# Layer 0's recurrence: the scan's input product on GpSimd beside a 1024-element sum, and the key softmax finished first

## The chip, the cores and the metric

The kernel runs on one core of one Trainium2 chip. The metric is the device time of one execution in microseconds (us); before the change the median of three runs is 1492.85 us (1488.32 to 1498.87). The five engines of a core run their own instruction streams and meet at semaphores: PE (TensorE, with PEld its weight loads), DVE (VectorE), ACT (ScalarE), POOL (GpSimd) and SP (which issues DMAs).

## The reference, cut to what matters

Two layers, each a mixer and a mixture of experts (MoE), on `[8, 512, 128]` float32. The change lies in the mixer of layer 0, a recurrence over 32 chunks of 16 tokens. Each of the 8 x 16 = 128 pairs of batch and head has two small weight matrices, `W_in` and `W_out`, of 4 x 8 elements, which are carried from chunk to chunk:

```
k_h = softmax_D(k_t . W_in) * lr_t[..., 1:]
q_h = softmax_D(q_t . W_in)
o_t = q_h . W_out + (mask(q_h k_h^T)) v_t
W_out = W_out + sum_n k_h[n] v[n]
for _ in range(2):
    g_out = -attn(W_in, k_t, v_t)
    g_in  = -attn(W_out, v_t, k_t)
    W_in  = W_in  - lr_in  * g_in
    W_out = W_out - lr_out * g_out
```

The masked product and `q_h . W_out` together are `q_h` times the running sum of `W_out + k_h v` over the tokens of the chunk, so the kernel makes a scan over the products `k_h v` and never forms the 16 x 16 matrix. After the recurrence come a layer norm per head, a gate, an output projection, the gathered result of the MoE, and layer 1.

## The kernel before, in words

The 128 pairs of batch and head lie on the 128 partitions. All of a chunk's work is on the free axis: 4 states (D) x 8 elements (e) x 16 tokens (l) = 512 elements, and 1024 where two weight matrices are taken as a pair.

One chunk is one call of `step(c, ...)` in the DVE block. It runs c = 0 alone, then three loops (c = 1, 2; c = 3 to 26; c = 27 to 30), then c = 31 alone. The 24 steps of the middle loop are called routed: during them PE and ACT also compute layer 0's MoE, three 128-token tiles a step, and DVE makes one 128x512 product for each tile (L1534, `gated`). In the routed steps GpSimd makes two of the recurrence's products, `q_product` (PQ, L446) and `o_product` (OP, L451), each 128x512. In the other eight steps DVE makes both itself, because GpSimd is issuing the indirect DMAs that scatter the MoE's input (L640, during c = 0 to 2) or gather its output (L675, from c = 27).

Order within DVE is kept by a counter, the class `Order`: `o.mark(...)` lets an instruction raise the counter when done and returns its number, `o.wait(n)` waits for that number. So an instruction whose operand has just been made waits for the instruction before it, and one that is independent of it is issued at once. Values that other engines make or need have semaphores of their own.

The part of a step that the change touches is its opening, up to the scan. The names are those of the code:

- `z_3` (L1542): sums of the pair's exponentials E3, 128 to 8 elements. `g_3` (L1547): the pair's product G3 = VV * E3, 1024 elements. `z_k` (L1549): sums of the key exponentials EK, 64 to 16 elements. `r_3`, `r_k` (L1551, L1553): reciprocals.
- `s_3` (L1555): the sum over the 1024 elements of G3 into 64 of GR. `l_k` (L1557): 16 elements of ZK times the learning rate. `n_3` (L1559): the 64 sums times the reciprocals Z3. `h_k` (L1561): EK times ZK, which finishes the key softmax.
- `w_c` (L1566): the new `W_out` into the first column of SC. `x_k` (L1568): the scan's input product V * EK, 512 elements, into the other 16 columns of each row of SC. `run` (L1571): the scan over SC, 544 elements, into CS.

After the scan the step computes the pair of scores with the new `W_out` (L1605 to L1611), the query softmax, the pair for `W_in` (L1615 to L1632), the scores for the next chunk (L1636 to L1644). Three gated products lie between. The exponentials are made on ACT (L1140), E3 before EK. The function `red` is DVE's tensor_reduce, `tt` its tensor_tensor, and `bc` makes a broadcast view.

GpSimd's stream in the routed steps is a loop: `o_product(c)`, then `q_product(c + 1)`. It waits for the query softmax of chunk c and then for the product at L1636, which DVE makes with the scores of chunk c + 1.

Of the kernel before, what the change touches and what calls it, by code (L numbers as in the profile page):

```python
# [9 lines left out]
ALU = mybir.AluOpType  # L10
ACT = mybir.ActivationFunctionType
AX_X = mybir.AxisListType.X

P = 128
B, L, D = 8, 512, 128
# [3 lines left out]
H, HD, DI, CH = 16, 8, 4, 16  # L19
# [13 lines left out]
FIRST = 3  # L33
# [5 lines left out]
def bc(ap, axis, n):  # L39

    a = ap.unsqueeze(axis)
    shape = list(a.shape)
    shape[axis] = n
    return a.broadcast_to(shape)

def flat(a):

    return a if len(a.shape) == 2 else a.rearrange("p a b -> p (a b)") if len(a.shape) == 3 else a.rearrange("p a b c -> p (a b c)")
# [55 lines left out]
def build(nc, d):  # L105
# [5 lines left out]
    with ExitStack() as ctx:  # L111
        def sb(name, shape, dt=F32):
            return ctx.enter_context(nc.sbuf_tensor(name, shape, dt))

        def sem(name):
            return ctx.enter_context(nc.semaphore(name))
# [41 lines left out]
        V = sb("V", [P, HD, L])  # L158
# [37 lines left out]
        G2, G3 = (r.take(2 * DI, HD, CH) for _ in range(2))  # L196
# [5 lines left out]
        SC, CS = r.take(DI * HD, CH + 1), r.take(DI * HD, CH + 1)  # L202
        EK, EQ = r.take(DI, CH), r.take(DI, CH)
        VV = r.take(2, HD * CH)
# [3 lines left out]
        S2, S3, E2, E3 = (r.take(2 * DI, CH) for _ in range(4))  # L208
# [5 lines left out]
        MK, MQ, ZK, ZQ = (sb(n, [P, CH]) for n in ("MK", "MQ", "ZK", "ZQ"))  # L214
        M2, M3, Z2, Z3 = (sb(n, [P, 2 * DI]) for n in ("M2", "M3", "Z2", "Z3"))
        GR = sb("GR", [P, 4, DI * HD])
# [90 lines left out]
        v_pair = sem("v_pair")  # L307
# [3 lines left out]
        op_ready = sem("op_ready")  # L311
        p3_ready = sem("p3_ready")
        qh_ready = sem("qh_ready")
        o_ps = sem("o_ps")
        o_copied = sem("o_copied")
        xg_loaded = [sem(f"xg_loaded{k}") for k in range(TPS)]
# [127 lines left out]
        def pq_of(eng, c):  # L444

            return eng.tensor_tensor(PQ, bc(Q[:, :, bass.ds(c * CH, CH)], 2, DI),  # L446
                                     bc(WI[:, 1, :].rearrange("p (D e) -> p e D", D=DI), 3, CH), ALU.mult)

        def op_of(eng):

            return eng.tensor_tensor(OP, bc(EQ, 2, HD), CS.rearrange("p (D e) l -> p D e l", D=DI)[:, :, :, 1:CH + 1], ALU.mult)  # L451
# [157 lines left out]
        def _(pool):  # L609
            o = Order(pool, pool_order)  # L610
# [41 lines left out]
            def q_product(c):  # L652

                pool.wait_ge(p3_ready, c)
                pool.wait_ge(q_ps, c)
                pq_of(pool, c).then_inc(pq_ready, 1)

            def o_product(c):

                pool.wait_ge(qh_ready, c + 1)
                pool.wait_ge(o_ps, c + 1)
                op_of(pool).then_inc(op_ready, 1)

            q_product(FIRST)
            with pool.Fori(FIRST, AFTER - 1) as c:
                o_product(c)
                q_product(c + 1)
            o_product(AFTER - 1)  # L670

            def gather(lo, hi):
# [693 lines left out]
        def _(dve):  # L1366
            o = Order(dve, dve_order)
            tt = dve.tensor_tensor
# [135 lines left out]
            red = dve.tensor_reduce  # L1504
            over_D = lambda a: a.rearrange("p D l -> p l D")
            state = lambda a: a.rearrange("p (D e) -> p D e", D=DI)
            both = lambda a: a.rearrange("p j (D e) -> p (j D) e", D=DI)
            SK = S3[:, DI:2 * DI, :]
            steps_of = lambda a: a.rearrange("p (D e) l -> p D e l", D=DI)
# [12 lines left out]
            def step(c, routed, first=False, last=False):  # L1522
                ts = bass.ds(c * CH, CH)
                kc, vc = K[:, :, ts], V[:, :, ts]
# [12 lines left out]
                if not routed:  # L1537
                    pq_of(dve, c).then_inc(pq_ready, 1)

                dve.wait_ge(exp_3, c + 1)  # L1540
                j = DI if first else 0
                z_3 = o.mark(red(Z3[:, j:], E3[:, j:], AX_X, ALU.add))  # L1542
                if first:
                    g_3 = o.mark(tt(G3[:, DI:], bc(vc, 1, DI), bc(E3[:, DI:], 2, HD), ALU.mult))
                else:
                    dve.wait_ge(v_pair, c)
                    g_3 = o.mark(tt(G3, bc(VV, 2, DI), bc(E3, 2, HD), ALU.mult))  # L1547
                dve.wait_ge(exp_k, c + 1)
                z_k = o.mark(red(ZK[:], over_D(EK), AX_X, ALU.add))  # L1549
                o.wait(z_3)  # L1550
                r_3 = o.mark(dve.reciprocal(Z3[:, j:], Z3[:, j:]))  # L1551
                o.wait(z_k)
                r_k = o.mark(dve.reciprocal(ZK[:], ZK[:]))  # L1553
                o.wait(g_3)
                s_3 = o.mark(red(both(GR[:, 2:4])[:, j:], G3[:, j:], AX_X, ALU.add))  # L1555
                o.wait(r_k)
                l_k = o.mark(tt(ZK[:], ZK[:], LR[:, 1, ts], ALU.mult))  # L1557
                o.wait(s_3)
                n_3 = o.mark(tt(both(GR[:, 2:4])[:, j:], both(GR[:, 2:4])[:, j:], bc(Z3[:, j:], 2, HD), ALU.mult))  # L1559
                o.wait(l_k)  # L1560
                h_k = o.mark(tt(EK, EK, bc(ZK[:], 1, DI), ALU.mult))  # L1561
                o.wait(n_3)
                if first:
                    w_c = o.mark(dve.tensor_copy(SC[:, :, 0], X[:, DI * HD:2 * DI * HD]))
                else:
                    w_c = o.mark(dve.scalar_tensor_tensor(SC[:, :, 0], GR[:, 2], lr_of(1, c - 1), WO[:, 1, :], ALU.mult, ALU.add))  # L1566
                o.wait(h_k)
                x_k = o.mark(tt(steps_of(SC)[:, :, :, 1:CH + 1], bc(vc, 1, DI), bc(EK, 2, HD), ALU.mult))  # L1568
                dve.wait_ge(op_ready, c + 1)
                o.wait(x_k)  # L1570
                run = o.mark(dve.tensor_tensor_scan(flat(CS), flat(seg[:]), flat(SC), 0.0, ALU.mult, ALU.add))  # L1571

                def q_softmax():
# [64 lines left out]
                s_3 = o.mark(red(S3, PP, AX_X, ALU.add))  # L1638
# [6 lines left out]
                gated(2)  # L1645

            PER_R = PER_P = 30
            step(0, False, first=True)
            for lo, hi, routed in ((1, FIRST, False), (FIRST, AFTER, True), (AFTER, NCH - 1, False)):  # L1650
                first, per = o.total(), PER_R if routed else PER_P
                with dve.Fori(lo, hi) as c:
                    o.loop(c, first - lo * per, per)
                    step(c, routed)
                o.end(first, per, hi - lo)
            step(NCH - 1, False, last=True)
            o.wait()

# [186 lines left out]
```

## Time and profile before

| | |
|---|---|
| median of 3 runs | 1492.85 us (1488.32 to 1498.87) |
| the profiled execution, its own time | 1495.63 us |
| its span, first to last instruction | 1493.9 us |
| DVE busy | 1299.2 us, 87% of the span |
| PE busy | 966.4 us, 65% |
| ACT busy | 694.7 us, 47% |
| POOL busy | 672.7 us, 45% |

The page's line of DVE's busy share in 40 slices of 37.3 us reads 9 (90% or more) or 8 through the whole recurrence, which runs from about 164 to 781 us. Busy times of consecutive DVE instructions overlap by some hundredths of a microsecond in the trace, so what an instruction costs in a stream is read from one start to the next. The rows that the prediction uses come in a section of their own below.

### The profile page before, as it was taken

The numbers are of one execution on the slowest core, as the hardware profiler recorded it, in microseconds if no ns is written. First come the engines' busy times: TensorE is split into PE (matmuls) and PEld (weight loads), VectorE is DVE, ScalarE is ACT, GpSimd is POOL, SyncE is SP. The second block draws the span as 40 slices with busy tenths as digits, with TensorE's granted clock in tenths as the row PEclk, the third lists the DMA queues.
The fourth block names the chain that finished last, engine by engine and source line by source line (L and its number), as shares of the span: only waits on it lengthen the run. The fifth ranks groups of instructions, "written<-read, shape, count | busy, mean of one in ns | idle before, by whom it ended". The sixth has DMA issues, their size and how long they took to land. (4 is left out here: it accounts for less than half of the span.)

```text
span 1493.9 us, 16154 instructions
## 1 busy us (share of the span) xinstructions
PE 966.4 (65%) x3484; PEld 565.0 (38%) x3485; DVE 1299.2 (87%) x2438; ACT 694.7 (47%) x1319; POOL 672.7 (45%) x609
## 2 busy tenths in 40 slices
PE   4760216877877777777330254667988889898652
PEld 2130214555555555555230251223444444443211
DVE  6768968999999999999988754899998988989995
ACT  3533203445555455553102021745776767767335
POOL 4004870111111011011754003774988979889774
PEclk9875557889899899897555656888999999999785
DMA  9993110000000000000114400544454445434474
GB/s 369 223 180 52 37 49 23 19 19 21 19 21 21 19 21 19 21 19 14 42 37 106 123 1 25 195 129 150 160 188 143 172 146 185 162 131 162 154 121 86
DMA packets 82990, 141.48 MB, mean 95 GB/s; under 512 B 12565, under 2 KB 54302, under 8 KB 78336
## 3 DMA queue, kind: packets, MB, share of 16 engines
q1 hardware_dynamic: 72512, 118.46, 26.3%
q0 software_dynamic: 10432, 22.52, 5.9%
q8 instruction: 15, 0.25, 0.1%
q14 instruction: 31, 0.25, 0.1%
HBM read 107.95 MB, written 34.60 MB: 95 GB/s over the span
## 5 line engine op out<-in xcount | busy, mean ns | idle before, releaser
L1736 DVE TENSOR_TENSOR ps<-ps,cv 128x512 f32<-128x512 f32 x256 | 162.5, 678 | 27.1 <-ACT ps L1323 27.1
L451 POOL TENSOR_TENSOR x<-x 128x512 f32<-128x512 f32 x24 | 28.4, 1183 | 344.9 <-DVE x L1587 344.9
L959 PE MATMUL ps<-Q,ident 128*128 128x512 f32 x256 | 142.4, 649 | 51.7 <-DVE Q L1754 38.4
L717 POOL TENSOR_TENSOR Q<-LR,xn 128x512 f32<-128x512 f32 x96 | 122.0, 1270 | 60.6 <-DVE LR L1745 45.3
L640 POOL DMA_INDIRECT slots_x<-xn,sl_put x64 | 74.4, 1163 | 130.4 <-DVE sl_put L1443 111.2
L835 PE MATMUL ps<-wd_a,xn 128*128 x576 | 99.5, 325 | 36.7 <-ACT xn L1123 36.7
L698 POOL DMA_INDIRECT slots_x<-xn,sl_put x64 | 64.2, 1003 | 128.7 <-issue 128.7
L845 PE MATMUL ps<-x,ident 128*128 128x64 f32 x512 | 76.5, 304 | 64.8 <-DVE x L446 58.5
L845 PEld LDWEIGHTS ps<-x,ident 128*128 128x128 f32 x512 | 75.7, 224 | 79.2 <-DVE x L446 66.8
L835 PEld LDWEIGHTS ps<-wd_a,xn 128*128 128x128 f32 x576 | 84.3, 225 | 49.6 <-issue 48.2
L818 PE MATMUL ps<-wg_a,xnT 128*128 x144 | 94.8, 746 | 12.2 <-issue 11.2
L1140 ACT ACTIVATE x<-x 128x128 f32<-128x128 f32 (+1 forms) x127 | 31.9, 276 | 138.2 <-DVE x L1611 60.8
L959 PEld LDWEIGHTS ps<-Q,ident 128*128 128x128 f32 x256 | 47.5, 201 | 128.0 <-DVE Q L1754 58.4
L1115 ACT ACTIVATE xnT<-ps 128x128 f32<-128x128 f32 x72 | 19.6, 272 | 145.0 <-PE ps L811 145.0
L853 PE MATMUL ps<-x,ident 128*128 128x128 f32 x256 | 45.0, 333 | 60.7 <-DVE x L451 60.5
L819 PE MATMUL ps<-wu_a,xnT 128*128 x144 | 83.2, 663 | 0.0
L825 PE MATMUL ps<-ident,xn 128*128 128x128 f32 x288 | 45.9, 283 | 52.6 <-DVE xn L1534 52.6
L1745 DVE TENSOR_TENSOR_SCAN LR<-V,ps 128x512 f32<-128x512 f32 x64 | 77.2, 1206 | 0.0
L1745 DVE TENSOR_TENSOR_SCAN LR<-wd_a,ps 128x512 f32<-128x512 f32 x64 | 77.1, 1205 | 0.0
L1745 DVE TENSOR_TENSOR_SCAN Q<-V,ps 128x512 f32<-128x512 f32 x64 | 76.1, 1190 | 0.0
L1745 DVE TENSOR_TENSOR_SCAN Q<-wd_a,ps 128x512 f32<-128x512 f32 x64 | 76.0, 1188 | 0.0
L853 PEld LDWEIGHTS ps<-x,ident 128*128 128x128 f32 x256 | 44.3, 248 | 79.6 <-DVE x L451 62.3
(303 smaller groups left out, 2809.7 us busy)
## 6 DMA issues: line engine op xcount, KB each, us to landing
cv<-bc_scr SPq DMA_DIRECT2D x64, 512.0 KB, 3.7
xn<-bc_scr SPq DMA_DIRECT2D x28, 1024.0 KB, 4.6
slots_x<-O POOLq DMA_DIRECT2D x28, 256.0 KB, 11.8
qkv_scr<-cv SPq DMA_DIRECT2D x24, 256.0 KB, 6.5
xnT<-slots_x SPq DMA_DIRECT2D x72, 64.0 KB, 1.7
slots_y<-xnT SPq DMA_DIRECT2D x72, 64.0 KB, 1.5
x<-in_x SPq DMA_DIRECT2D x8, 512.0 KB, 5.8
O<-bc_scr SPq DMA_DIRECT2D x4, 1024.0 KB, 6.0
```

Source lines behind the costliest of these rows:

```text
L640: pool.indirect_dma_start(out=slots_x, out_offset=bass.IndirectOffsetOnAxis(ap=sl_put[:, j, i:i + 1], axis=0), in_=xn[:, i, :], in_offset= ...
L698: pool.indirect_dma_start(out=slots_x1, out_offset=bass.IndirectOffsetOnAxis(ap=sl_put[:, j, i:i + 1], axis=0), in_=xn[:, i, :], in_offset ...
L717: pool.tensor_tensor(yc_g0[:, n % 4, :], st_g0[:, n % 2, :], cn, ALU.mult).then_inc(yc_ready, 1)
L818: pe.matmul(ps[:, 1 + 2 * k, :], xgT[:, k, :], wg_a[:, bass.ds(off, F)], start=True, stop=True).then_inc(gu_ps, 1)
L819: pe.matmul(ps[:, 2 + 2 * k, :], xgT[:, k, :], wu_a[:, bass.ds(off, F)], start=True, stop=True).then_inc(gu_ps, 1)
L825: t = pe.transpose(ps[:, 1 + 2 * k, f * P:(f + 1) * P], hid[:, k, f * P:(f + 1) * P], ident[:])
L835: m = pe.matmul(ps[:, 0, 0:D], hidT[:, k, f * P:(f + 1) * P], wd_a[:, bass.ds(off + f * D, D)], start=(f == 0), stop=(f == FC - 1))
L845: m = pe.matmul(ps[:, 7, 0:DI * CH], ident[:], PQ[:, e, :, :], start=(e == 0), stop=(e == HD - 1))
L853: m = pe.matmul(ps[:, 7, 0:HD * CH], ident[:], OP[:, r, :, :], start=(r == 0), stop=(r == DI - 1))
L959: pe.matmul(ps[:, 4, :], ident[:], yc_g0[:, n % 4, :], start=(n == 0), stop=(n == NS - 1)).then_inc(y0_used, 1)
L1736: tt(dBu(g), ps[:, 2 + g, :], b_rows[:, n % 4, :], ALU.mult).then_inc((inject0, b_used)[g], 1)
L1745: dve.tensor_tensor_scan(st(n, g), dA(k), dBu(g), 0.0, ALU.mult, ALU.add).then_inc(scanned, 1)
```

## The change

In the DVE block the opening of every step gets a new order. The key softmax (`z_k`, `r_k`, `l_k`, `h_k`) is finished ahead of the pair's product G3, and `h_k` raises a semaphore `kh_ready`; G3 raises `g3_ready`, for which DVE itself waits before `s_3`. In the routed steps DVE no longer makes `x_k`: GpSimd does, in a new function `k_product`, after `kh_ready` and `g3_ready`, and raises `xk_ready`. In the eight other steps DVE makes it at the old place, ahead of the scan. The scan waits for `xk_ready` and now also for `w_c` by name. GpSimd's loop becomes `o_product(c)`, `q_product(c + 1)`, `k_product(c + 1)`. The counter's marks per step (PER_R, PER_P) fall from 30 to 27, since three instructions raise semaphores of their own.

```
+        g3_ready = sem("g3_ready")
+        kh_ready = sem("kh_ready")
+        xk_ready = sem("xk_ready")
...
+        def xk_of(eng, c):
+            return eng.tensor_tensor(SC.rearrange("p (D e) l -> p D e l", D=DI)[:, :, :, 1:CH + 1],
+                                     bc(V[:, :, bass.ds(c * CH, CH)], 1, DI), bc(EK, 2, HD), ALU.mult)
...
+            def k_product(c):
+                pool.wait_ge(kh_ready, c + 1)
+                pool.wait_ge(g3_ready, c + 1)
+                xk_of(pool, c).then_inc(xk_ready, 1)
+
             q_product(FIRST)
+            k_product(FIRST)
             with pool.Fori(FIRST, AFTER - 1) as c:
                 o_product(c)
                 q_product(c + 1)
+                k_product(c + 1)
...
                 z_3 = o.mark(red(Z3[:, j:], E3[:, j:], AX_X, ALU.add))
-                if first:
-                    g_3 = o.mark(tt(G3[:, DI:], bc(vc, 1, DI), bc(E3[:, DI:], 2, HD), ALU.mult))
-                else:
-                    dve.wait_ge(v_pair, c)
-                    g_3 = o.mark(tt(G3, bc(VV, 2, DI), bc(E3, 2, HD), ALU.mult))
                 dve.wait_ge(exp_k, c + 1)
                 z_k = o.mark(red(ZK[:], over_D(EK), AX_X, ALU.add))
                 o.wait(z_3)
                 r_3 = o.mark(dve.reciprocal(Z3[:, j:], Z3[:, j:]))
                 o.wait(z_k)
                 r_k = o.mark(dve.reciprocal(ZK[:], ZK[:]))
-                o.wait(g_3)
-                s_3 = o.mark(red(both(GR[:, 2:4])[:, j:], G3[:, j:], AX_X, ALU.add))
                 o.wait(r_k)
                 l_k = o.mark(tt(ZK[:], ZK[:], LR[:, 1, ts], ALU.mult))
+                o.wait(l_k)
+                tt(EK, EK, bc(ZK[:], 1, DI), ALU.mult).then_inc(kh_ready, 1)
+                if first:
+                    tt(G3[:, DI:], bc(vc, 1, DI), bc(E3[:, DI:], 2, HD), ALU.mult).then_inc(g3_ready, 1)
+                else:
+                    dve.wait_ge(v_pair, c)
+                    tt(G3, bc(VV, 2, DI), bc(E3, 2, HD), ALU.mult).then_inc(g3_ready, 1)
+                dve.wait_ge(g3_ready, c + 1)
+                s_3 = o.mark(red(both(GR[:, 2:4])[:, j:], G3[:, j:], AX_X, ALU.add))
                 o.wait(s_3)
                 n_3 = o.mark(tt(both(GR[:, 2:4])[:, j:], both(GR[:, 2:4])[:, j:], bc(Z3[:, j:], 2, HD), ALU.mult))
-                o.wait(l_k)
-                h_k = o.mark(tt(EK, EK, bc(ZK[:], 1, DI), ALU.mult))
                 o.wait(n_3)
...
-                o.wait(h_k)
-                x_k = o.mark(tt(steps_of(SC)[:, :, :, 1:CH + 1], bc(vc, 1, DI), bc(EK, 2, HD), ALU.mult))
+                if not routed:
+                    dve.wait_ge(kh_ready, c + 1)
+                    xk_of(dve, c).then_inc(xk_ready, 1)
                 dve.wait_ge(op_ready, c + 1)
-                o.wait(x_k)
+                o.wait(w_c)
+                dve.wait_ge(xk_ready, c + 1)
                 run = o.mark(dve.tensor_tensor_scan(flat(CS), flat(seg[:]), flat(SC), 0.0, ALU.mult, ALU.add))
...
-            PER_R = PER_P = 30
+            PER_R = PER_P = 27
```

## Rows read from the trace of the kernel before

**Rows 1.** Two stretches: length, busy PE, PEld, DVE, ACT, POOL, clock, DMA, GB/s.
```profile
238.91:704.24 465.33, 364.38 (x1784) 255.44 (x1784) 439.82 (x938) 228.18 (x521) 53.73 (x47) 0.89 0.07 19
704.24:777.89 73.65, 22.98 (x96) 21.08 (x96) 70.57 (x152) 8.53 (x30) 48.88 (x44) 0.53 0.13 39
```

**Rows 2.** DVE in order of time, opening of chunk 21: start, duration, line, operation.
```profile
583.30 0.28 DVE L1542 TENSOR_REDUCE Z<-x 128x8 f32<-128x128 f32 x1
583.50 1.22 DVE L1547 TENSOR_TENSOR cv<-x 128x1024 f32<-128x1024 f32 x1
584.63 0.26 DVE L1549 TENSOR_REDUCE ZK<-x 128x16 f32<-128x64 f32 x1
584.80 0.20 DVE L1551 RECIPROCAL Z<-Z 128x8 f32<-128x8 f32 x1
584.92 0.25 DVE L1553 RECIPROCAL ZK<-ZK 128x16 f32<-128x16 f32 x1
585.09 1.16 DVE L1555 TENSOR_REDUCE GR<-cv 128x64 f32<-128x1024 f32 x1
586.17 0.16 DVE L1557 TENSOR_TENSOR ZK<-ZK,LR 128x16 f32<-128x16 f32 x1
586.28 0.23 DVE L1559 TENSOR_TENSOR GR<-GR,Z 128x64 f32<-128x64 f32 x1
586.43 0.22 DVE L1561 TENSOR_TENSOR x<-x,ZK 128x64 f32<-128x64 f32 x1
586.68 0.27 DVE L1566 SCALAR_TENSOR_TENSOR x<-GR,LR,WO 128x32 f32<-128x32 f32 x1
586.89 0.69 DVE L1568 TENSOR_TENSOR x<-V,x 128x512 f32<-128x512 f32 x1
587.61 1.29 DVE L1571 TENSOR_TENSOR_SCAN x<-seg,x 128x544 f32<-128x544 f32 x1
```

**Rows 3.** DVE in order of time, later in chunk 20.
```profile
576.58 0.23 DVE L1587 TENSOR_TENSOR x<-x,ZQ 128x64 f32<-128x64 f32 x1
...
578.44 0.22 DVE L1627 TENSOR_TENSOR GR<-GR,Z 128x64 f32<-128x64 f32 x1
578.79 0.25 DVE L1629 SCALAR_TENSOR_TENSOR WI<-GR,LR,WI 128x32 f32<-128x32 f32 x1
...
579.36 1.22 DVE L1636 TENSOR_TENSOR x<-wproj,WI 128x1024 f32<-128x1024 f32 x1
```

**Rows 4.** POOL in order of time, chunk 20; the bracket is idle time and its releaser.
```profile
576.88 1.18 POOL L451 TENSOR_TENSOR x<-x 128x512 f32<-128x512 f32 x1 [15.31 <-DVE x L1587]
580.77 1.10 POOL L446 TENSOR_TENSOR x<-Q,WI 128x512 f32<-128x512 f32 x1 [2.71 <-DVE x L1636]
```

**Rows 5.** One line's instructions, layer 1's products on POOL: ns min/median/max.
```profile
L717 POOL TENSOR_TENSOR Q<-LR,xn x96: 1257/1270/1288, 1025.0 to 1386.4; 128x512 f32<-128x512 f32 x96
```

**Rows 6.** DVE in order of time, layer 1, beside rows 7.
```profile
999.42 5.68 DVE L1756 TENSOR_TENSOR seg<-Q,O 128x512 f32<-128x512 f32 x1
```

**Rows 7.** POOL in order of time, layer 1; each row is two products back to back.
```profile
999.59 2.52 POOL L704 TENSOR_TENSOR gateT<-gateT,V 128x512 f32<-128x512 f32 x2
1002.04 2.50 POOL L708 TENSOR_TENSOR gateT<-gateT 128x512 f32<-128x512 f32 x2
```

**Rows 8.** DVE's waits, routed steps (234 to 704.3 us): total us, times, longest.
```profile
DVE Z L1542 <- ACT x L1140: 7.3, 10, 1.0
DVE Z L1615 <- ACT x L1140: 2.9, 10, 0.3
```

**Rows 9.** PE in order of time, chunks 21 and 22: the same eight matmuls twice.
```profile
587.08 1.15 PE L835 MATMUL ps<-wd_a,xn 128*128 x8
...
613.91 2.07 PE L835 MATMUL ps<-wd_a,xn 128*128 x8 [0.77 <-ACT xn L1123]
```

**Rows 10.** DVE in order of time, chunk 2, the wait ahead of the query's sum.
```profile
227.42 0.26 DVE L1581 TENSOR_REDUCE ZQ<-x 128x16 f32<-128x64 f32 x1 [13.68 <-ACT x L1140]
```

**Rows 11.** POOL in order of time, the last of the 64 scattering DMAs.
```profile
222.43 0.95 POOL L640 DMA_INDIRECT slots_x<-xn,sl_put  x1 [0.30 <-issue]
```

## The prediction

> **What bounds the kernel now.** I read the busy shares first, then the stretch of the recurrence by itself, then DVE's instructions in order of time, then the waits of DVE and the POOL rows. From chunk 3's scan to chunk 27's, DVE is busy for 439.8 of 465.3 us, where POOL is busy for 53.7; from there to the last scan it is 70.6 of 73.65 [rows 1]. So the recurrence is one stream of DVE instructions, and what counts is their starts. In the opening of a step [rows 2] the reader is to see two spacings. Where the next instruction is independent, it starts before the last one's row ends: L1549 to L1551 is 0.17 us for a duration of 0.26. Where it needs the last one's result, it starts about 0.03 after that one's end: L1568 ends at 587.58, the scan starts at 587.61. The old order mixes two independent chains, the pair's and the key's, so nearly every instruction has the cheap spacing. The scan starts 4.31 after L1542.
>
> **The new order, routed steps.** Times are from the start of `z_3`; all durations stay those of [rows 2]. `z_3` 0; `z_k` 0.20 (the step that L1542 now gives L1547); `r_3` 0.37; `r_k` 0.49. Now comes what the mixing hid: `l_k` needs `r_k`: 0.49 + 0.25 + 0.03 = 0.77. `h_k` needs `l_k`: 0.77 + 0.16 + 0.03 = 0.96. G3 is independent of it: 0.96 + 0.15 (as L1559 to L1561) = 1.11. `s_3` needs G3: 1.11 + 1.22 + 0.03 = 2.36. `n_3` needs `s_3`: 2.36 + 1.16 + 0.03 = 3.55. `w_c` needs `n_3`; the same pair of operations one after the other is L1627 to L1629, 0.35 [rows 3], so 3.90. The scan needs `w_c`: 3.90 + 0.27 + 0.03 = 4.20. Taking away `x_k` is worth 0.72 (L1568 to L1571), and the exposed latencies eat 0.61 of it: 4.31 becomes 4.20, if nothing else is in the way.
>
> **GpSimd's product.** Its place is after G3's end at 2.33. L446 on POOL starts at 580.77, 0.19 after the end of L1636 at 580.58, which is the same kind of instruction as G3 [rows 3, 4]; L451 starts 0.07 after the end of L1587 at 576.81 [rows 3, 4]. I take 0.19, since `k_product`, like `q_product`, reads a chunk at an address of the loop's variable. POOL makes 512 products in 1.10 or 1.18 us in this recurrence [rows 4] and in 1.27 in layer 1 [rows 5]; no row shows this one, and 1.10 and 1.27 are the ends. I take 1.18, as L451 walks the same 17-column rows (it reads CS; `x_k` writes SC). So it runs from 2.52 to 3.70, ahead of the scan's 4.20: the move itself is hidden, behind `s_3`, `n_3` and `w_c`. If it were not, each 0.1 us past 4.20 would cost 2.4 us in all. POOL has nothing queued behind it but `o_product(c)`, which waits for the query softmax: L451 came 15.3 us after POOL's last work [rows 4]. SP issues nothing new.
>
> **The edge of the overlap.** The product ends 0.15 after `n_3` could start, and `n_3` is a tensor_tensor with two operands in SBUF. What that means the trace does show, in layer 1: DVE's L1756, such an instruction, takes 5.68 us (other rows of that line have 0.69) beside four products of POOL, and ends at 1005.10, 0.56 after the last of these ends at 1004.54 [rows 6, 7]. DVE was shut out until POOL was done. But 0.56 is 0.13 less than 0.69, so a held instruction has its front behind it when it is let go. For `n_3` (0.22) I take the same: it ends 3.70 + 0.10 = 3.80 in place of 3.77, and the scan starts at 4.23, 0.08 earlier than before. `s_3` is a reduction with one operand; L1638 of the same size runs beside POOL's L446 already, so I charge it nothing. Bounds: no hold at all gives 4.20 (-0.11 a step); a hold in which `n_3` too ends 0.56 after a product of 1.27 (at 3.79) ends it at 4.35 and gives a scan at 4.35 + 0.13 + 0.30 = 4.78 (+0.47). Over 24 routed steps: -1.9 us, from -2.6 to +11.3.
>
> The page SBUF — State Buffer of the Trainium skill says (section SBUF: two separate sides) that GpSimd and a DVE instruction with two SBUF inputs take a shared pair of ports as an exclusive lock, for the whole instruction; another section, A bandwidth-pool intuition that's wrong, has the loser wait until the holder's end plus about 115 ns. Rows 6 and 7 agree with the lock, and not with a full instruction after the release. By the page `n_3` would end at 3.70 + 0.115 + 0.22 = 4.035, the scan start at 4.465, and the routed steps lose 0.155 x 24 = 3.7 us, an estimate: 1499 in place of the number below.
>
> **The eight steps in which DVE keeps the product.** They get the new order and no relief. `w_c` is at 3.90, `x_k` follows 0.21 later (as L1566 to L1568), the scan 0.72 after that: 4.83 against 4.31, +0.52. In chunks 27 to 31 that is on the path: DVE was busy for 96% of that stretch [rows 1], and POOL's gathers are released by DVE itself. 5 x 0.52 = +2.6 us; bounds +2.2 (if the 0.35 were 0.26) and +3.0. In chunks 0 to 2 it costs nothing: in chunk 2 DVE waits 13.68 us ahead of L1581 [rows 10], for ACT, which stands in its queue behind the first expert tile, which waits for POOL's scatter to end at 223.38 [rows 11]. Three openings of +0.52 fit. If that cover were gone they would add 1.6.
>
> **The sum.** -1.9 + 2.6 = +0.7 us. The profiled execution took 1495.63, of which 1493.9 is span, so its successor takes 1496.3; it stood 2.8 above the median of the three runs, so the median goes to 1492.85 + 0.7 = 1493.6. Bounds of the terms: 0 to +14.3.
>
> **Rivals.**
>
> The forecast, chance 0.56: the opening is nearly as long as it was, and the time stays at 1494. Its own range is 1489 to 1500, the scatter of the runs before.
>
> The clock, chance 0.16. In the routed steps DVE waits for ACT's exponentials, 7.3 us at L1542 and 2.9 at L1615, in ten steps each and not in the others [rows 8]. Behind it stands PE: the same eight matmuls take 1.15 in one step and 2.07 in the next [rows 9], since PE had idled before and the granted clock (0.89 in the mean [rows 1]) went to its lower level of 1.2 GHz. A step shorter by a tenth shifts PE's idle time against this. If the low clock missed the chain, all 10.2 us would go: 1483.4. If every step had such a wait (0.73 + 0.29 each), 24 x 1.02 - 10.2 = +14.3: 1508. That the waits come so regularly says that the pattern is stable; I give the better side 0.10, the worse 0.06. In part, the waits also swallow gains: in ten of 24 steps an earlier DVE waits longer.
>
> The hold, which makes it slower, chance 0.19. It decides at `n_3`: the scan is late as soon as `n_3` ends later than 3.88, that is 0.18 us behind POOL's product. A whole `n_3` after the release ends at 3.92: scan 4.35, +1.0 + 2.6 = +3.6, so 1496.5. By the upper bound it is +11.3 + 2.6 = +13.9: 1506.8. For it: the one row of a collision. Against: the product overlaps `n_3` by 0.15 us only, and if it takes 1.10 hardly at all.
>
> The product's whole worth, chance 0.06: the dependent spacings are hidden by something and every routed step gains 0.72, 17.3 - 2.6 = 14.7: 1478. Against it are the spacings of rows 2 and 3, which are the same in every step.
>
> The rest (0.03) is left for what I don't see.
>
> **How the numbers follow.** 1493.6 is the likeliest case's. The range runs from 1484 (the clock's better side; below it are the product's whole worth and little else) to 1505 (the hold up to near its bound; above it the clock's worse side). About 1%, 15 us, is what a measurement of this kernel can tell from no change: below 1478 lies half of the last rival and a little scatter, 0.04; above 1508 lie half of the clock's worse side and the end of the hold, 0.06; the rest, 0.90, is within.
>
> **What would show it.** Right: in routed rows `z_3` to scan takes 4.2 to 4.3 us, `l_k`, `h_k`, `n_3` each start only after the one before has ended, POOL's new line runs some 1.1 to 1.2 us from 2.5 on, and the five last openings take 4.8. The hold shows as an `n_3` or `w_c` of more than 0.3 us, or a row of `n_3` that ends well behind POOL's. The clock shows in the waits at `z_3` and the pair's second sum: their total moves away from 10.2. Wrong: a scan that starts below 4.0, a wait of DVE for POOL ahead of the scan, or chunks 0 to 2 that lengthen the stretch before chunk 3's first instruction.

## The result and the profile after

The changed kernel takes 1505.01 us (median of 8 runs, 1498.95 to 1506.81), the kernel before 1493.45 (8 runs beside them): ratio 1.0066, 95% interval 1.0043 to 1.0088. That is +0.7%: the kernel became slower, by less than 1% but clear of no change. The median lies on the upper end of the forecast's range (1505), whose likeliest value was +0.7 us and not +11.6. The profiled execution took 1500.19 us, with a span of 1498.4.

The recurrence holds the loss. Its last scan starts at 788.27 us in place of 777.89, 10.4 later. Behind that scan the code is the same in both kernels and the profiled executions scatter: it takes 716.0 us before and 710.1 here, and 707.9 to 717.4 in four further traces, which is why the two spans are only 4.5 us apart. The two stretches of [rows 1], in the changed kernel (length, busy PE, PEld, DVE, ACT, POOL, granted clock, DMA share, GB/s):

```profile
239.55:711.58 472.03, 375.17 (x1784) 260.36 (x1784) 436.76 (x914) 227.68 (x521) 82.92 (x70) 0.86 0.07 19
711.58:788.27 76.69, 22.97 (x96) 21.07 (x96) 72.03 (x153) 8.49 (x30) 46.28 (x44) 0.51 0.14 37
```

The routed stretch grew by 6.7 us, the last four steps by 3.0. DVE is busy for 3.1 us less in the routed stretch and the stretch is longer: what DVE gave away came back as gaps. They can be seen in the opening of chunk 21 in the changed kernel, DVE in order of time, the answer to [rows 2]:

```profile
589.06 0.28 DVE L1559 TENSOR_REDUCE Z<-x 128x8 f32<-128x128 f32 x1 [0.80 <-ACT x L1157]
589.26 0.25 DVE L1561 TENSOR_REDUCE ZK<-x 128x16 f32<-128x64 f32 x1
589.43 0.19 DVE L1563 RECIPROCAL Z<-Z 128x8 f32<-128x8 f32 x1
589.58 0.25 DVE L1565 RECIPROCAL ZK<-ZK 128x16 f32<-128x16 f32 x1
590.00 0.18 DVE L1567 TENSOR_TENSOR ZK<-ZK,LR 128x16 f32<-128x16 f32 x1 [0.16 <-DVE ZK L1565]
590.21 0.23 DVE L1569 TENSOR_TENSOR x<-x,ZK 128x64 f32<-128x64 f32 x1
590.35 1.22 DVE L1574 TENSOR_TENSOR cv<-x 128x1024 f32<-128x1024 f32 x1
591.60 1.22 DVE L1576 TENSOR_REDUCE GR<-cv 128x64 f32<-128x1024 f32 x1
592.86 0.28 DVE L1578 TENSOR_TENSOR GR<-GR,Z 128x64 f32<-128x64 f32 x1
593.30 0.28 DVE L1583 SCALAR_TENSOR_TENSOR x<-GR,LR,WO 128x32 f32<-128x32 f32 x1 [0.17 <-DVE GR L1578]
593.61 1.29 DVE L1590 TENSOR_TENSOR_SCAN x<-seg,x 128x544 f32<-128x544 f32 x1
```

From the first sum to the scan it is 4.55 us, where it was 4.31 and 4.23 were forecast. Two gaps are large enough to be listed as waits: 0.16 us ahead of L1567 (`l_k`) and 0.17 ahead of L1583 (`w_c`). GpSimd's product is in its forecast place beside the sum, POOL in order of time:

```profile
591.79 1.26 POOL L454 TENSOR_TENSOR x<-V,x 128x512 f32<-128x512 f32 x1 [5.04 <-DVE cv L1574]
```

It ends at 593.05, 0.56 ahead of the scan: the scan never waits for it. DVE's listed waits in the routed steps, the answer to [rows 8] (total us, times, longest):

```profile
DVE Z L1559 <- ACT x L1157: 9.6, 13, 0.9
DVE x L1583 <- DVE GR L1578: 4.2, 25, 0.2
DVE ZK L1567 <- DVE ZK L1565: 3.9, 24, 0.2
```

The wait for ACT is 9.6 us in all, where it was 10.2. The other two are new. The list leaves out gaps of about 0.15 us and less; taken from the spacing of the rows, as is done below the table at the end of the experiments, the waits for ACT rose a little, from 11.7 to 12.6 us.

The steps in which DVE keeps the product, chunk 30 in the loop, DVE in order of time:

```profile
764.38 0.28 DVE L1559 TENSOR_REDUCE Z<-x 128x8 f32<-128x128 f32 x1
...
764.86 0.25 DVE L1565 RECIPROCAL ZK<-ZK 128x16 f32<-128x16 f32 x1
765.26 0.17 DVE L1567 TENSOR_TENSOR ZK<-ZK,LR 128x16 f32<-128x16 f32 x1
...
768.12 0.22 DVE L1578 TENSOR_TENSOR GR<-GR,Z 128x64 f32<-128x64 f32 x1
768.51 0.27 DVE L1583 SCALAR_TENSOR_TENSOR x<-GR,LR,WO 128x32 f32<-128x32 f32 x1 [0.17 <-DVE GR L1578]
...
769.47 1.29 DVE L1590 TENSOR_TENSOR_SCAN x<-seg,x 128x544 f32<-128x544 f32 x1
```

and chunk 31, which is written out after the loop, so that no address depends on a loop's variable:

```profile
783.88 0.25 DVE L1565 RECIPROCAL ZK<-ZK 128x16 f32<-128x16 f32 x1
784.16 0.17 DVE L1567 TENSOR_TENSOR ZK<-ZK,LR 128x16 f32<-128x16 f32 x1
...
787.02 0.22 DVE L1578 TENSOR_TENSOR GR<-GR,Z 128x64 f32<-128x64 f32 x1
787.28 0.27 DVE L1583 SCALAR_TENSOR_TENSOR x<-GR,LR,WO 128x32 f32<-128x32 f32 x1
```

The reader is to compare the spacings. From the key's reciprocal to `l_k` it is 0.40 in the loop and 0.28 out of it, from `n_3` to `w_c` 0.39 and 0.26. The same instructions on operands of the same shape cost 0.12 and 0.13 more where the learning rate is read at an address that the loop's variable gives. That is the lead for the first theory.

In chunk 2, DVE's wait ahead of the query's sum shrank to 9.86 from the 13.68 of [rows 10] and still covers the openings of chunks 0 to 2:

```profile
227.63 0.26 DVE L1600 TENSOR_REDUCE ZQ<-x 128x16 f32<-128x64 f32 x1 [9.86 <-ACT x L1157]
```

### The profile page after: what moved, and what is told of

The parts are those of the page before. It is cut to its first block and busy times, and to the rows that moved or that the text cites. A ratio compares the mean times of both kernels' runs of the same rounds, so it can differ in the third digit from the quotient of the medians.

```text
span 1498.4 us, 16170 instructions
## 1 busy us (share of the span) xinstructions
PE 970.8 (65%) x3484; PEld 565.8 (38%) x3485; DVE 1295.9 (86%) x2414; ACT 694.2 (46%) x1319; POOL 700.0 (47%) x633
## 5 line engine op out<-in xcount | busy, mean ns | idle before, releaser
L835 PE MATMUL ps<-wg_a,xnT 128*128 x144 | 98.8, 776 | 10.9 <-issue 9.5
L836 PE MATMUL ps<-wu_a,xnT 128*128 x144 | 87.5, 695 | 0.0
L454 POOL TENSOR_TENSOR x<-V,x 128x512 f32<-128x512 f32 x24 | 30.4, 1266 | 110.2 <-DVE cv L1574 110.2
```

Of the source, the lines that this page charges most:

```text
L835: pe.matmul(ps[:, 1 + 2 * k, :], xgT[:, k, :], wg_a[:, bass.ds(off, F)], start=True, stop=True).then_inc(gu_ps, 1)
L836: pe.matmul(ps[:, 2 + 2 * k, :], xgT[:, k, :], wu_a[:, bass.ds(off, F)], start=True, stop=True).then_inc(gu_ps, 1)
```

## The experiments

Three theories stood against each other. **Order:** the loss is latency on DVE itself, which the old order hid and the new one exposes, in its sharper form the making of addresses behind a wait. **GpSimd:** the product on GpSimd slows the DVE instructions beside it. **Clock:** the routed steps meet PE's lower clock in another way, so that DVE waits longer for ACT. Ratios are with the kernel before, run beside them on the same chip. Beside the first four experiments it took 1554.58 us, beside the last three 1550.15 and beside the four between 1491.39. The recurrence takes as long on the slower chip as on the first (the changed kernel's routed stretch is 472.03 and 472.20 us), and what takes longer lies behind it (767 to 777 us behind the last scan in place of 708 to 717). So the stretches of all runs can be compared, and the times only within a group. Below, "opening" is the time from `z_3` to the scan in the routed steps and "routed stretch" the time from chunk 3's scan to chunk 27's, both from one profiled execution of each kernel.

**The order alone.** The new order everywhere, the product on DVE everywhere.

```
             q_product(FIRST)
-            k_product(FIRST)
...
-                if not routed:
-                    dve.wait_ge(kh_ready, c + 1)
-                    xk_of(dve, c).then_inc(xk_ready, 1)
+                dve.wait_ge(kh_ready, c + 1)
+                xk_of(dve, c).then_inc(xk_ready, 1)
```

> The new order in all 32 steps, but DVE makes the scan's input product in all of them; GpSimd keeps only its two old products. Order theory (the loss is latency that the new order exposes on DVE): the routed opening, first sum to scan, becomes that of the changed kernel's last steps, 5.1 us, 0.8 above before, and the time rises by 24 x 0.8 + 5 x 0.8 = 23 us over before, to 1516. GpSimd theory (the product on GpSimd slows DVE's sum, scaling and column beside it): the opening gets back most of the 0.3 that the routed steps lost against the forecast and stands near 4.8, and the time near 1508. In both the row of the 64-element scaling tells the hold: 0.22 us here, 0.29 in the changed kernel.

Measured: ratio 1.0171 (1.0113 to 1.0228). The opening is 5.15 us, routed stretch 492.27. With no product on GpSimd beside them, the sum still takes 1.22 and the two waits are there as before, DVE in order of time:

```profile
585.31 0.25 DVE L1563 RECIPROCAL ZK<-ZK 128x16 f32<-128x16 f32 x1
585.73 0.17 DVE L1565 TENSOR_TENSOR ZK<-ZK,LR 128x16 f32<-128x16 f32 x1 [0.17 <-DVE ZK L1563]
...
587.33 1.22 DVE L1574 TENSOR_REDUCE GR<-cv 128x64 f32<-128x1024 f32 x1
588.59 0.23 DVE L1576 TENSOR_TENSOR GR<-GR,Z 128x64 f32<-128x64 f32 x1
588.98 0.28 DVE L1581 SCALAR_TENSOR_TENSOR x<-GR,LR,WO 128x32 f32<-128x32 f32 x1 [0.17 <-DVE GR L1576]
```

The new order costs 0.84 us a step, and the move gives 0.60 of it back. GpSimd's product shows only in the scaling, 0.28 us beside it against 0.23 here. But the stretch grew by 26.9, more than 24 x 0.84 = 20.2: the waits for ACT rose to 17.1 us, in all 24 steps. Length alone isn't the whole story.

**The move alone.** The old order, the product on GpSimd in the routed steps.

```
+                if routed:
+                    h.then_inc(kh_ready, 1)
...
+                if routed:
+                    o.wait(w_c)
+                    dve.wait_ge(xk_ready, c - (FIRST - 1))
```

> The old order in all steps; in the 24 routed ones GpSimd makes the scan's input product as soon as the key softmax is finished, which the old order does at 3.35 us of the opening. Order theory: the product runs from 3.55 to 4.8 with nothing of use beside it, the scan starts near 4.9 to 5.0, +0.65 a routed step, about 1508 (+15). GpSimd theory: still later, since the new first column of the scan, an instruction with two operands in SBUF, collides with the product in full: scan near 5.3, 1517.

Measured: ratio 1.0102 (1.0041 to 1.0163), opening 4.81, routed stretch 480.65. DVE's waits in the routed steps:

```profile
DVE x L1593 <- POOL x L453: 26.6, 23, 1.2
```

Here the scan does wait for GpSimd, 1.16 us a step, more than the 0.72 that the product costs on DVE. The product is late, as the order theory had it, and the opening 0.1 shorter than it said. So the key softmax must come first, and that order must not cost what it saves.

**The eight other steps as before.** The routed steps keep the change's order, the others get their old one.

```
+                if routed:
+                    (the opening of the changed kernel)
+                else:
+                    (the opening of the kernel before)
```

> The routed steps as in the changed kernel, the eight others as before the change. Both theories: the routed opening stays at 4.55, the last five go back to 4.3, and the time falls by 5 x 0.77 = 3.8 us against the changed kernel, to about 1501, still 7 above before. If chunks 0 to 2 cost something after all, it falls by up to 2.3 more. Clock theory (the loss is in how the routed steps meet PE's low clock): the total of the routed stretch moves by more than 1 us though its instructions are the same.

Measured: ratio 1.0016 (0.9986 to 1.0045), routed opening 4.52, the last openings 4.30, stretches 469.56 and 73.70 (before: 465.33 and 73.65). The last steps' 3.0 us are gone, as expected. The routed stretch is 2.5 shorter too: it ends with the scan of chunk 27, in which DVE keeps the product, and that opening is back at 4.30 from 5.08; the 23 others, 0.03 shorter each, make 0.7, and the waits, by spacing, 1.1.

**The 1024-element product between the reciprocal and its use.** One edit to the kernel of the experiment above, in the routed steps.

```
                     r_k = o.mark(dve.reciprocal(ZK[:], ZK[:]))
+                    dve.wait_ge(v_pair, c)
+                    tt(G3, bc(VV, 2, DI), bc(E3, 2, HD), ALU.mult).then_inc(g3_ready, 1)
                     o.wait(r_k)
                     l_k = o.mark(tt(ZK[:], ZK[:], LR[:, 1, ts], ALU.mult))
                     o.wait(l_k)
                     tt(EK, EK, bc(ZK[:], 1, DI), ALU.mult).then_inc(kh_ready, 1)
-                    dve.wait_ge(v_pair, c)
-                    tt(G3, bc(VV, 2, DI), bc(E3, 2, HD), ALU.mult).then_inc(g3_ready, 1)
```

> As the run before it, but in the routed steps the pair's 1024-element product stands between the key's reciprocal and its scaling by the learning rate, so that it covers that latency. Order theory: 0.25 of the 0.31 us come back; the key softmax ends at 2.25, GpSimd's product runs 2.45 to 3.7, the scaling of the sums, ready at 3.45, is held to 3.8, scan at 4.3: as before, time 1493 to 1495. GpSimd theory: the longer hold (0.25 in place of 0.07) costs more than it shows in the product's end: scan at 4.5 or later, 1499 or more.

Measured: ratio 0.9919 (0.9885 to 0.9954), 1540.33 against 1554.58 us. It is 0.8% faster than the kernel before, where no gain was expected. Opening 4.14 (4.3 expected), routed stretch 454.39. DVE, then POOL, in order of time:

```profile
593.72 0.25 DVE L1563 RECIPROCAL ZK<-ZK 128x16 f32<-128x16 f32 x1
593.89 1.16 DVE L1565 TENSOR_TENSOR cv<-x 128x1024 f32<-128x1024 f32 x1
594.97 0.16 DVE L1567 TENSOR_TENSOR ZK<-ZK,LR 128x16 f32<-128x16 f32 x1
595.16 0.23 DVE L1569 TENSOR_TENSOR x<-x,ZK 128x64 f32<-128x64 f32 x1
595.31 1.21 DVE L1571 TENSOR_REDUCE GR<-cv 128x64 f32<-128x1024 f32 x1
596.55 0.36 DVE L1573 TENSOR_TENSOR GR<-GR,Z 128x64 f32<-128x64 f32 x1
597.08 0.27 DVE L1575 SCALAR_TENSOR_TENSOR x<-GR,LR,WO 128x32 f32<-128x32 f32 x1 [0.17 <-DVE GR L1573]
```
```profile
595.55 1.28 POOL L454 TENSOR_TENSOR x<-V,x 128x512 f32<-128x512 f32 x1 [3.75 <-DVE x L1569]
```

The wait ahead of `l_k` is gone. The hold (the scaling `n_3`, stopped while GpSimd's product runs) is longer, 0.36 us in place of 0.22, and still cheap: `n_3` ends at 596.91, 0.08 behind the product's end at 596.83. Yet 0.17 us of opening in 24 steps are 4.1, and the stretch fell by 10.9. The rest is in the waits for ACT, listed with 3.3 us in all where they were 10.2:

```profile
DVE Z L1655 <- ACT x L1155: 1.9, 5, 0.5
DVE Z L1557 <- ACT x L1155: 1.3, 3, 0.5
```

**Fixed addresses.** The changed kernel, with both learning rates read from chunk 0 always.

```
-                l_k = o.mark(tt(ZK[:], ZK[:], LR[:, 1, ts], ALU.mult))
+                l_k = o.mark(tt(ZK[:], ZK[:], LR[:, 1, 0:CH], ALU.mult))
...
-  ... GR[:, 2], lr_of(1, c - 1), WO[:, 1, :] ...
+  ... GR[:, 2], LR[:, 1, 0:1], WO[:, 1, :] ...
```

> The changed kernel, with the learning rates of the scaling l_k and of the column w_c read from chunk 0 always (so the output differs), which takes the loop's variable out of their addresses. Order theory in its sharper form (behind each wait, an instruction whose address depends on the loop's variable also waits for the register work that makes the address): l_k starts 0.28 us after the key's reciprocal in place of 0.42, w_c 0.1 earlier behind n_3, opening 4.3 in place of 4.55. If those 0.14 and 0.1 are plain latency of the data, nothing moves. GpSimd theory: nothing moves.

Measured, in one execution: opening 4.25, in the last steps 4.84 in place of 5.08. DVE in order of time:

```profile
581.35 0.25 DVE L1565 RECIPROCAL ZK<-ZK 128x16 f32<-128x16 f32 x1
581.64 0.17 DVE L1567 TENSOR_TENSOR ZK<-ZK,LR 128x16 f32<-128x16 f32 x1
...
584.49 0.28 DVE L1578 TENSOR_TENSOR GR<-GR,Z 128x64 f32<-128x64 f32 x1
584.81 0.27 DVE L1583 SCALAR_TENSOR_TENSOR x<-GR,LR,WO 128x32 f32<-128x32 f32 x1
```

Reciprocal to `l_k` 0.29 in place of 0.42, `n_3` to `w_c` 0.32 in place of 0.44. The data dependences are what they were; only the addresses became constant. This is shown: in the loop, each of the two instructions paid about 0.13 us for its address, behind the wait that stands ahead of it. The opening is then within 0.02 of the forecast's 4.23. The execution took 1491.96 us, beside 1491.39 for the kernel before: in that one execution the loss is gone. The routed stretch is 459.18, 12.9 less than in the changed kernel, and the openings make only 7.0 of it; the waits for ACT, by spacing, fell from 12.6 to 5.9 us and make the rest, to within 0.8.

**A quarter of the product.** The changed kernel, GpSimd computing 128 of the 512 elements.

```
-                xk_of(pool, c).then_inc(xk_ready, 1)
+                pool.tensor_tensor(SC...[:, 0:1, :, 1:CH + 1], bc(V..., 1, 1),
+                                   bc(EK[:, 0:1], 2, HD), ALU.mult).then_inc(xk_ready, 1)
```

> The changed kernel, but GpSimd computes only a quarter of the scan's input product (128 of 512 elements; the others stay as they were, so the output differs). It is done before the sum over the pair's product is. Order theory with a small hold: n_3 goes from 0.28 to 0.22, the sum s_3 stays at 1.22, opening 4.55 to 4.48. GpSimd theory: the sum is shorter too and the opening falls by 0.2 or more, to under 4.35.

Measured, in one execution: the product takes 0.45 us; the sum beside it 1.22 as before, the scaling 0.22, opening 4.49. With the full product the scaling is 0.28. So the hold is 0.06 us a step, 1.4 in all, and the sum isn't slowed. The GpSimd theory falls, but for this. The execution took 1505.61 us, so the loss stays.

**The kernel before, made longer.** One unread sum of 0.20 us more in each routed step.

```
                 z_3 = o.mark(red(Z3[:, j:], E3[:, j:], AX_X, ALU.add))
+                if routed:
+                    red(spare[:], E3, AX_X, ALU.add)
```

> The kernel before the change with one more DVE sum in the routed steps, whose result nobody reads, 0.20 us of spacing in the opening. Plain-length theory (a routed step costs what DVE's stream is long, and the waits for ACT stay at 10 us): 24 x 0.20 = +4.8 us in the routed stretch. Clock theory (the waits for ACT behind PE's low clock depend on how the step's length stands to the clock's rhythm): the stretch moves by more or less than that by 2 us or more, since the waits' total changes.

Measured: ratio 1.0045 (1.0028 to 1.0062), opening 4.51, routed stretch 469.63 (+4.3), waits for ACT 8.4 us as listed and 11.7 by spacing, as before. 24 x 0.20 is 4.8 (23 x 0.20 is 4.6, since chunk 27's opening has no extra sum). The plain length carries this one: the difference of 0.5 is under the 2 that the clock theory had asked for.

**The faster kernel, made longer.** The same unread sum in the kernel with the product between.

```
                     z_3 = o.mark(red(Z3[:], E3, AX_X, ALU.add))
+                    red(spare[:], E3, AX_X, ALU.add)
```

> The kernel with the 1024-element product between reciprocal and scaling, with the same unread sum of 0.20 us added in its routed steps: opening 4.34, as before the change (4.31). It had 454.4 us from the scan of chunk 3 to that of chunk 27, where before the change it was 465.3, and waits of 3.3 us in place of 10.2. Plain-length theory: +4.8, 459. Clock theory: the gain of that kernel beyond its shorter opening came from missing the low clock, and a step as long as before brings the waits back: 465, +10.

Measured: ratio 1.0014 (0.9988 to 1.0039), opening 4.33, routed stretch 465.13, the clock theory's 465 and not the plain length's 459. The stretch by itself, then the waits:

```profile
237.65:702.78 465.13, 364.09 (x1784) 255.16 (x1784) 435.24 (x937) 227.94 (x521) 82.93 (x70) 0.89 0.07 19
```
```profile
DVE Z L1558 <- ACT x L1156: 7.1, 10, 0.9
DVE Z L1657 <- ACT x L1156: 2.9, 10, 0.3
```

These are the figures of the kernel before, nearly to the digit: 465.33 us, clock 0.89, waits of 7.3 and 2.9. The kernel without the extra sum has this row:

```profile
237.55:691.94 454.39, 346.03 (x1784) 242.99 (x1784) 430.65 (x915) 228.41 (x521) 83.01 (x70) 0.93 0.07 20
```

24 x 0.19 us are 4.6, the difference is 10.7. PE runs the same 1784 matmuls in 364 us in the one and 346 in the other, at a granted clock of 0.89 and 0.93. So a part of the gain of 10.9 us was never in the opening: with a step 0.17 us shorter PE shows the low clock less often, and DVE waits 6.8 us less. That the length of the step decides over these waits is shown by the one sum put in; that they come by way of PE's clock is read from these rows, where clock, PE's busy time and waits move together, and was not tested by itself.

**One more fixed address.** The kernel with the product between; ACT copies the learning rate that `w_c` needs to one place, a step earlier.

```
+  act.activation(LC[:], LR[:, 1, bass.ds(c * CH, 1)], ACT.Copy).then_inc(lc_ready, 1)
...
-  ... GR[:, 2], lr_of(1, c - 1), WO[:, 1, :] ...
+  ... GR[:, 2], LC[:, 0:1], WO[:, 1, :] ...
```

> The kernel with the 1024-element product between reciprocal and scaling, in whose routed steps w_c also takes its learning rate from one fixed place, where ACT has copied it a step earlier (0.2 us of ACT a step). Address theory: w_c starts 0.12 us earlier behind n_3, opening 4.02 in place of 4.14. Plain-length theory: 24 x 0.12 = 2.9 us less in the routed stretch, 451.5. Clock theory: the stretch moves by another amount; with steps that alternate between 18.68 and 18.87 us now and PE as the likely other holder of that rhythm, the waits take the gain back and it stays at 454.

Measured: ratio 0.9886 (0.9804 to 0.9967), opening 4.01, routed stretch 452.27, waits for ACT 4.9 us. The 0.13 us come off the opening; the stretch falls by 2.1 of the 3.1 that they make, between what the plain length (451.5) and the clock theory (454) had asked for. Between this and the kernel with the product between the ratios don't decide (0.9924 beside it); its one trace is 1.3 and 2.1 us shorter than the two of that kernel, which differ by 0.8 themselves.

**Both again, on one chip.** The changed kernel and the one with the product between.

> The changed kernel as it is, on the same chip as the two beside it. All theories: ratio to before 1.006 to 1.008, routed stretch 472, opening 4.55.

> The kernel with the 1024-element product between reciprocal and scaling, again, beside the changed kernel on one chip. If its rhythm of steps is its own and not luck of one execution: routed stretch 454 to 457 and ratio to before 0.992; if luck, the stretch stands at 460 to 466 and the ratio at 0.998 or above.

Measured: the changed kernel 1.0098 (1.0058 to 1.0139), routed stretch 472.20, opening 4.55; the other 0.9924 (0.9886 to 0.9963), 453.60, opening 4.14. A second execution gives the changed kernel's stretch to 0.2 us and the other's to 0.8. The rhythm is the kernel's own: from about the tenth routed step on, its steps alternate between 18.69 and 18.87 us in both executions.

**All of it in one sum.** Routed stretch = 465.33 + 24 x (opening - 4.31) + (listed waits for ACT - 10.2). The last two columns are explained below the table.

| kernel | opening | listed waits | by the sum | measured | waits by spacing | by the rows |
|---|---|---|---|---|---|---|
| fixed rate | 4.01 | 4.9 | 452.8 | 452.27 | 5.8 | 452.4 |
| product between | 4.14 | 3.3 | 454.4 | 454.39 | 4.9 | 454.6 |
| fixed addresses | 4.25 | 5.5 | 459.2 | 459.18 | 5.9 | 458.7 |
| between, longer | 4.33 | 10.0 | 465.6 | 465.13 | 11.4 | 465.4 |
| a quarter of the product | 4.49 | 8.6 | 468.1 | 470.40 | 12.1 | 470.6 |
| before, longer | 4.51 | 8.4 | 468.3 | 469.63 | 11.7 | 469.7 |
| eight others as before | 4.52 | 8.4 | 468.6 | 469.56 | 11.5 | 469.7 |
| changed | 4.55 | 9.6 | 470.5 | 472.03 | 12.6 | 472.3 |
| move alone | 4.81 | 14.7 | 481.8 | 480.65 | 15.8 | 480.9 |
| order alone | 5.15 | 17.1 | 492.4 | 492.27 | 18.6 | 492.3 |

The sum holds within 0.6 us for five of the ten; the others are 1.0 to 2.3 above it, the move alone 1.2 below. Two things are missing from it. The 24th opening of the stretch is chunk 27's, in which DVE keeps the product: 5.08 us in the changed kernel and not 4.55. And the list of waits leaves out small gaps: from the first gated product to the pair's second sum (`z_2`) it is 0.75 us in chunk 20 (578.73 to 579.48), where 0.60 is the spacing without a wait. The last two columns take the 24 openings from their own rows, and the waits as the spacing above 0.60 us ahead of `z_2` and `z_3` in each step (11.7 us before the change). That sum meets all ten stretches within 0.3 us, but for 0.5 in the fixed addresses: what changed from one kernel to the next is the openings and the waits for ACT, and hardly anything else. It also shows where the waits move: they are 11 us or more in every kernel whose opening is 4.31 or longer, and 4.9 to 5.9 in the three whose opening is 4.25 or shorter.

## Why the prediction was eleven microseconds low, at the edge of its range

**The forecast's case** was that the exposed latencies eat nearly all of what moving the product saves. Such latencies there were, but they ate more than all of it: 0.72 us went and 0.96 came. The size was wrong by 0.32 us a routed step, and with it the sign: the routed openings were to be 0.08 shorter and are 0.24 longer, the routed stretch 6.7 us longer where 1.9 less was forecast. That 1505.01 still lies at the range's end is luck, since the range reached that far for the hold and the clock, and neither did this.

**The step that failed** is the chain of spacings in the new order, above all the latency ahead of `l_k`, in the words of the prediction "`l_k` needs `r_k`: 0.49 + 0.25 + 0.03 = 0.77" and "all durations stay those of [rows 2]". `l_k` starts at 0.94, and not because of the data. The gap of 0.03 was read from instructions whose address is ready when their wait ends. `l_k` reads the learning rates at an address made from the loop's variable, and in that order it is made after the wait: 0.13 us, taken away by the fixed addresses. In the old order L1555, 1.16 us long, stood between them and hid it. The prediction knew of addresses on POOL, where it took 0.19 us for the start for that reason, and did not ask the same of DVE. For `w_c` it had the right pair, L1627 to L1629 [rows 3], and was off by 0.04 (0.39 without the hold, in a quarter of the product). Of the 0.32, `l_k` is 0.14, the sum's longer row 0.06 (1024-element rows show 1.16 us directly behind a reciprocal, as L1555 in [rows 2] and the product in the kernel with the product between, and 1.21 to 1.25 behind everything else), `w_c` and the hold ahead of it 0.06, small spacings the rest.

**GpSimd's product** was placed right: it starts 0.22 us behind the 1024-element product's end (0.19 forecast; 0.14 in chunk 3, where it stands outside GpSimd's loop), and the scan never waits for it. It takes 1.27 us, the upper bound, and not 1.18.

**The hold** exists and is as small as [rows 6, 7] had it: the scaling ends 0.09 behind the product's end in the changed kernel (593.14 against 593.05), 0.08 in the kernel with the longer overlap. The forecast had 0.10. The Trainium skill's page SBUF — State Buffer (section A bandwidth-pool intuition that's wrong) gives about 115 ns past the holder's end, for a DMA issued by GpSimd behind a copy on DVE; with a whole `n_3` after it, the prediction's estimate, it would be 0.34. These traces agree with the exclusive lock of the page's section SBUF: two separate sides, and not with that price. As a rival the hold is out; all of it is worth 0.06 us a step.

**The other steps** had the sign and 0.25 us too little: 5.08 in place of 4.83, from the same address of `l_k` and the same longer sum. On the path they cost 3.0 us in chunks 28 to 31 (0.66 of it in the last) and 0.8 in chunk 27, whose opening is counted in the routed stretch: 3.8 for all five, where 2.6 was said. Chunks 0 to 2 cost nothing, as said: their cover shrank from 13.68 to 9.86 us and held.

**The clock** did not move much in the change itself: the waits stood at 9.6 us by the list that the prediction used. But the prediction's sentence that a shorter step could miss the low clock is what the kernel with the product between shows, -6.9 us of waits, two thirds of the price that was put on it. It was given 0.10 for a step shorter by 0.08. The runs say that this was too little: in the kernel with fixed addresses, whose opening is 0.06 shorter than before and nearly the forecast's, the waits fall from 11.7 to 5.9 us. Had the opening been the 4.23 of the forecast, the time would likely have fallen by several us and not stayed; one trace says so.

**A slip in the sum:** the lower bound of the terms is -2.6 + 2.2 = -0.4, not 0. Nothing hangs on it.

## What to carry to other kernels

Moving an instruction to another engine is worth its spacing only if what stood between dependent instructions still does. Count the new neighbours: each dependent pair costs its data latency (0.03 us behind the end of the row here), and in a loop another 0.13 us if the second one's address comes from the loop's variable and its wait stands in front of it. A long independent instruction belongs exactly there, as the 1024-element product between the reciprocal and `l_k` shows. Where another engine's clock or waits beat against the length of a step, test a small change of length by itself before a gain or loss is put down to the edit.

## What the runs showed of the hardware that was not expected

- The steps of the routed stretch don't lengthen evenly. The kernel before repeats 19.25, 18.87 and 19.9 us, the changed one four steps of 19.25, 19.10, 20.04 and 20.12, the order alone stands at 20.48 from the seventh step on, the one with the product between alternates between 18.69 and 18.87. What makes the chip fall to the low clock in one of these and not in the other stays open: the runs show the granted clock (0.83 for the order alone, 0.86 changed, 0.89 before, 0.93 with the product between), not what it answers to.
- A small DVE instruction that wants both operands from SBUF and meets GpSimd's product shows a longer row, and ends 0.07 to 0.09 us behind the product, whether it had stood for 0.06 us or for 0.14: `n_3` (64 elements) in all held steps. The 512-element L1756 of [rows 6] ends 0.56 behind.
- A start ahead of GpSimd's product does not always keep a DVE instruction from the hold; one case shows it. In the move alone `w_c` starts 0.13 us ahead of it in 23 steps and keeps its 0.27 us. In chunk 3, whose product stands outside GpSimd's loop and comes earlier, `w_c` starts 0.05 ahead and is held to 0.07 behind the product's end:

```profile
235.75 1.38 DVE L1583 SCALAR_TENSOR_TENSOR x<-GR,LR,WO 128x32 f32<-128x32 f32 x1
235.80 1.26 POOL L453 TENSOR_TENSOR x<-V,x 128x512 f32<-128x512 f32 x1 [4.82 <-DVE x L1574]
```
